# One transformer layer on one core: scatters of routed rows issued earlier, and the first residual sum moved from VectorE to TensorE and ScalarE

## What is computed

```
att = softmax(einsum(zq, zk) / sqrt(rank));  y = (att @ zv) @ U.T
x   = layernorm(x + y @ Wo.T + bo)
top 2 of softmax(x @ gate_w.T), renormalised -> combine
h   = relu(x @ w1.T + b1);  expert_out = h @ w2.T + b2
out = layernorm(x + sum over experts of expert_out * combine)
```

## Time and profile before

| | |
|---|---|
| median of 3 runs | 1260.19 us (1258.29 to 1507.58) |
| the profiled execution's own time | 1257.38 us |
| its span in the trace | 1255.6 us |
| PE / DVE / ACT / POOL busy | 86% / 78% / 72% / 47% |
| attention part | up to about 906 us, bodies b = 0 to 15 |
| routing tail and table | about 906 to 944 us |
| expert part | 944 to 1212 us |
| final layer norms | 1212 to 1256 us |

### The profile page before, as it was taken

One profiled execution on the slowest core, in us unless ns is written; L12 is line 12 of the kernel. 1 busy time (PEld: TensorE's weight loads), 2 busy tenths in 40 slices (PEclk: granted clock), 3 DMA queues, 4 the chain that ended last, 5 costly groups with the idle time before them and its releaser, 6 DMA issues. The chain is left out here.

```text
span 1255.6 us, 24757 instructions
## 1 busy us (share of the span) xinstructions
PE 1082.8 (86%) x7711; PEld 520.5 (41%) x7711; DVE 975.3 (78%) x2117; ACT 904.2 (72%) x1177; POOL 586.5 (47%) x823
## 2 busy tenths in 40 slices
PE   3578998989889898898988999888728999999977
PEld 2222222222222222222222222222218999999952
DVE  4578888989778797887988879797146888888845
ACT  1157877778677786867878678687618999999927
POOL 1314316255271642626336263323254777777745
PEclk9989999999899998989999899899758999999989
DMA  3733133141331413223142231400012222222246
GB/s 80 235 94 90 49 101 89 54 132 42 95 92 51 126 37 106 73 67 102 43 127 69 71 97 36 122 15 19 14 51 63 69 68 69 69 69 71 66 159 257
DMA packets 105461, 104.88 MB, mean 84 GB/s; under 512 B 21608, under 2 KB 82834, under 8 KB 105376
## 3 DMA queue, kind: packets, MB, share of 16 engines
q1 hardware_dynamic: 94912, 81.88, 22.5%
q0 software_dynamic: 8448, 16.93, 4.2%
q10 hardware_dynamic: 2016, 4.98, 1.1%
HBM read 56.06 MB, written 47.39 MB: 82 GB/s over the span
## 5 line engine op out<-in xcount | busy, mean ns | idle before, releaser
L799 DVE TENSOR_REDUCE row_max<-score_ps 128x2 f32<-128x1024 f32 x512 | 618.0, 1220 | 138.9 <-PE score_ps L571 91.3
L685 ACT ACTIVATE probs<-score_ps 128x1024 f32<-128x1024 f32 x512 | 521.6, 1023 | 157.4 <-PE score_ps L553 132.6
L534 PE MATMUL av_ps<-probs,v_one 128*9 128x512 f32 x2048 | 285.2, 630 | 7.9 <-ACT probs L685 6.5
L571 PE MATMUL score_ps<-k_stack,q_stack 48*128 48x512 bf16 x1024 | 207.5, 402 | 75.2 <-ACT probs L685 57.5
L553 PE MATMUL score_ps<-q_stack,k_stack 51*128 51x512 bf16 x1024 | 205.7, 399 | 22.0 <-DVE row_max L799 15.1
L371 POOL TENSOR_TENSOR max_parts<-neg_max,zeros 32x128 bf16<-32x128 f32 x32 | 14.2, 445 | 386.9 <-ACT neg_max L623 386.9
L1096 ACT ACTIVATE w_cur<-experts 128x1156 f32 x136 | 158.5, 1167 | 37.5 <-PEq L413 17.2
L553 PEld LDWEIGHTS score_ps<-q_stack,k_stack 51*128 51x128 bf16 x1024 | 49.2, 93 | 320.4 <-issue 154.2
L1192 POOL DMA_INDIRECT y_d<-y_out,place x136 | 136.8, 1006 | 44.7 <-issue 44.7
L846 POOL DMA_INDIRECT routed_d<-rows,slot_i x128 | 125.4, 980 | 67.2 <-issue 36.9
L1053 PE MATMUL up_ps<-xt_sb,w_cur 128*128 128x128 f32 x1088 | 146.2, 278 | 0.0
(11 more groups left out here) (187 smaller groups left out, 1153.3 us busy)
## 6 DMA issues: line engine op xcount, KB each, us to landing
k_stack<-k_stack_d SPq DMA_DIRECT2D x128, 96.0 KB, 2.4
q_stack<-q_stack_d SPq DMA_DIRECT2D x128, 96.0 KB, 2.5
x_rows_sb<-routed_d SPq DMA_DIRECT2D x136, 65.0 KB
q_stack_d<-q_parts SPq DMA_DIRECT2D x32, 192.0 KB
k_stack_d<-k_parts SPq DMA_DIRECT2D x30, 192.0 KB
x_in<-L_attn_x SPq DMA_DIRECT2D x16, 256.0 KB, 3.1
q_stack_d<-q_parts SPq DMA_DIRECT2D x32, 128.0 KB
x_res<-L_attn_x SPq DMA_DIRECT2D x16, 256.0 KB, 3.1
```

Source lines behind the costliest of these rows:

```text
L534: last = nc.tensor.matmul(av_ps[32 * g:32 * g + V_COLS, :], v_one[n.parity][:, kb, HG * hg + g, :], probs[:, (2 * j + g // 2) % P_RING, g ...
L571: last = nc.tensor.matmul(max_bank(b, s)[:, a, :], q_stack[n.parity][at, c, g * P:(g + 1) * P], k_stack[n.parity][at, c, :], start=True, s ...
L685: nc.scalar.activation(probs[:, s % P_RING, :, :], exp_bank(b, s)[:, :, :], ACT.Exp).then_inc(S["exp_done"], 1)
L799: nc.vector.tensor_reduce(row_max[:, m // (STEPS // 2), :, m % (STEPS // 2)], max_bank(b, s)[:, :, :], AX.X, ALU.max).then_inc(S["red_done ...
```

## The change

Three edits, all in the attention part.

1. **Residual on PE.** At s = 11 PE waits for `xbo_ready` too, and each of the four output projections is followed by a matmul of the identity with `x_bo` into the same PSUM columns, so that the sum is made in `misc_ps`. A new function `residual` on ACT, at s = 12, copies `misc_ps` (128x512) to `res`. DVE's addition goes; its statistics move from s = 12 to s = 13 and the moments from s = 13 to s = 14.
2. **Scatters 0 and 1** of p2 move ahead of `split_max(b, 1)`.
3. **Scatters 2 to 7** of p2 come directly behind `split_max(b, 1)`, ahead of the layer norm's small operations and of `split_q` and `split_k` (where there is a current batch; in the last two bodies they stay at the end).

The diff:

```diff
--- before.py
+++ after.py
@@ -464,8 +464,10 @@
                             if s == 11 and prev:
                                 pe.wait_ge(S["ynt_sb"], p1.count(1, 1))
                                 emptied(s)
+                                pe.wait_ge(S["xbo_ready"], p1.count(1, 1))
                                 for t in range(QT):
-                                    last = nc.tensor.matmul(misc_ps[:, t * P:(t + 1) * P], y_t[:, t * P:(t + 1) * P], wo_t[:, :], start=True, stop=True)
+                                    nc.tensor.matmul(misc_ps[:, t * P:(t + 1) * P], y_t[:, t * P:(t + 1) * P], wo_t[:, :], start=True, stop=False)
+                                    last = nc.tensor.matmul(misc_ps[:, t * P:(t + 1) * P], ident[:, :], x_bo[:, t, :], start=False, stop=True)
                                 last.then_inc(S["wo_done"], 1)
                             if s == 17 and cur:
                                 emptied(s)
@@ -610,8 +612,14 @@
                             wait(act, S["yt_done"], n.count(HG, hg - 1))
                             nc.scalar.activation(y_sb[hg % 2][:, :], av_ps[:, :], ACT.Copy).then_inc(S["y_ready"], 1)
 
+                        def residual(n):
+                            act.wait_ge(S["wo_done"], n.count(1, 1))
+                            wait(act, S["x1_ready"], n.count(QT, 0))
+                            nc.scalar.activation(res[:, :, :].rearrange("p t d -> p (t d)"), misc_ps[:, :], ACT.Copy).then_inc(S["res_ready"], 1)
+
                         def scale_out(n, t):
                             if t == 0:
+                                act.wait_ge(S["res_ready"], n.count(1, 1))
                                 act.wait_ge(S["shift_ready"], n.count(1, 1))
                                 wait(act, scattered[n.parity], n.count_parity(8 * 16, 0))
                             nc.scalar.activation(rows[n.parity][:, 0, t, 0:D], res[:, t, :], ACT.Identity, bias=shift[:, t:t + 1],
@@ -659,6 +667,8 @@
                                 nc.scalar.activation(x1_t[:, :], misc_ps[:, :], ACT.Copy).then_inc(S["x1t_sb"], 1)
                             if s == 10 and cur:
                                 neg(b, 1)
+                            if s == 12 and prev:
+                                residual(p1)
                             if s == 20 and nxt:
                                 act.wait_ge(S["v_done"], n1.count(1, 1))
                                 wait(act, S["av_done"], b.count(STEPS // 2, 0))
@@ -701,11 +711,6 @@
                                                     inv_sum[:, hg, :, :].unsqueeze(3).to_broadcast([P, QT, HG, R]), ALU.mult).then_inc(S["yn_sb"], 1)
 
                         def layernorm(n):
-                            dve.wait_ge(S["wo_done"], n.count(1, 1))
-                            dve.wait_ge(S["xbo_ready"], n.count(1, 1))
-                            wait(dve, S["x1_ready"], n.count(QT, 0))
-                            nc.vector.tensor_tensor(res[:, :, :].rearrange("p t d -> p (t d)"), misc_ps[:, :],
-                                                    x_bo[:, :, :].rearrange("p t d -> p (t d)"), ALU.add).then_inc(S["res_ready"], 1)
                             dve.wait_ge(S["res_ready"], n.count(1, 1))
                             for t in range(QT):
                                 nc.vector.bn_stats(stats[:, t, :], res[:, t, :]).then_inc(S["stats_ready"], 1)
@@ -781,7 +786,7 @@
                                         route(p2, k)
                             if s == 4 and prev:
                                 y_normalise(p1, 3)
-                            if s == 12 and prev:
+                            if s == 13 and prev:
                                 layernorm(p1)
                             if s == 18 and cur:
                                 y_normalise(b, 0)
@@ -789,7 +794,7 @@
                                 y_normalise(b, 1)
                             if s == 30 and cur:
                                 y_normalise(b, 2)
-                            if s == 13 and prev:
+                            if s == 14 and prev:
                                 dve.wait_ge(S["stats_ready"], p1.count(QT, QT))
                             if maximum_at(b, s) is not None:
                                 n, m = Batch(0, maximum_at(b, s) // STEPS), maximum_at(b, s) % STEPS
@@ -853,17 +858,19 @@
                                            base=2 * T * p2.c, channel_multiplier=2).then_inc(S["place_out"], 1)
                         if prev:
                             pool.wait_ge(xres_loaded[p1.parity], p1.count_parity(16, 16))
-                            wait(pool, S["res_ready"], p1.count(1, 0))
+                            wait(pool, S["wo_done"], p1.count(1, 0))
                             nc.gpsimd.tensor_tensor(x_bo[:, :, :], x_res[p1.parity][:, :, :], bo_b[:, :].unsqueeze(1).to_broadcast([P, QT, D]),
                                                     ALU.add).then_inc(S["xbo_ready"], 1)
-                        if cur:
-                            split_max(b, 1)
                         if prev2:
                             pool.wait_ge(S["place_out"], p2.count(1, 1))
                             pool.wait_ge(S["top_step"], p2.count(TOP_STEPS, TOP_STEPS))
                             pool.wait_ge(S["slot_step"], p2.count(SLOT_STEPS, SLOT_STEPS))
                             pool.wait_ge(S["copied"], p2.count(1, 1))
                             scatter(p2, 0, 2)
+                        if cur:
+                            split_max(b, 1)
+                        if prev2 and cur:
+                            scatter(p2, 2, 8)
                         if prev:
                             pool.wait_ge(S["mv_ready"], p1.count(QT, QT))
                             nc.gpsimd.tensor_tensor(var_eps[:, :], mean_var[:, :, 1], eps_t[:, :], ALU.add).then_inc(S["vareps_ready"], 1)
@@ -877,12 +884,10 @@
                         if proj and not is_first(b):
                             split_q(nc.gpsimd, pool, n2)
                             split_k(nc.gpsimd, pool, n2)
-                        if prev2:
-                            scatter(p2, 2, 6)
                         if nxt:
                             split_max(n1, 0)
-                        if prev2:
-                            scatter(p2, 6, 8)
+                        if prev2 and not cur:
+                            scatter(p2, 2, 8)
 
                     schedule(pool, body)
```

## The result

The changed kernel takes 1286.8 us (median of 4 runs, 1282.6 to 1289.2), the kernel before 1261.4; the ratio is 1.021, with a 95% interval of 1.016 to 1.025. The 1261.4 is the median of four runs, one of which took 1507.6 us in a slower state of the chip and counts in no ratio. The forecast was 1286. That the total came out almost exactly is luck: several of its terms were wrong, and their errors cancelled. The profiled execution took 1282.6 us, 25.2 more than the one before.

The account below looks back on a forecast made before the run. The chain through POOL and SP was to bind: 53.0 us plus 1.6 of clock gives 54.6 for bodies 2 to 13, +21; with the other bodies and tail +28.5 on 1257.4, so 1286 us; 8-in-10 range 1261 to 1305.

Parts of the forecast that it names:

- POOL's slip of 3.45 us: POOL's queue behind the six scatters: `var_eps`, `shift`, the q and k parts and the k stores start 3.45 us later.
- The chain from k store to s = 0: From the k stores through SP's queue to the next body's s = 0, which waits for the maxima: 14.93 us.
- The 53.0 us by the chain: Period from s = 0 to s = 0 set by POOL and SP: 49.5 us plus the slip of 3.45.
- PE then sits idle for about 3.3 us at each s = 0: PE waits at s = 0 for the maxima: period 53.0 us less the body's own 49.7.
- PE's own way through the body: The body's own work without the pause: 49.0 us now, about 49.7 with the change, hidden under 53.0.
- I expect the pause at s = 25 to go: Engines' stop near s = 25, about 2.2 us, blamed on scatters running beside k stores; moved scatters would end it.
- rival B: Every s = 0 wait ends in the long clock fall, 3.2 us: 1305 us, chance 0.14; a pause moving with six scatters, nearly the same.
- Its sign for the clock: If PE's rows at s = 0 to 4 stay at 0.39 us, the clock term goes and 1270 us results.
- The clock, 1.6 us a body at s = 0: PE falls to half clock behind its wait at s = 0, lengthening the chain by 1.6 us, bounds 0 and 3.2.
- The sum: Against 1257.4 us: bodies 2 to 13 +21, body 1 +3.5, 14 and 15 +1 each, tail +2; +28.5, 1286 us.
- Residual on PE, +1.1 us, hidden: Four more 128x128 fp32 matmuls at s = 11 add 1.1 us on PE, hidden under the 53.0 us period.
- Rival C: Pause goes and the chain does not bind, so the period is 49.7 us: 1223 us, chance 0.06.

Follow-up runs that it names:

- spread orders: Two kernels: the kernel before with its eight scatters in four pairs, none ahead of the q and k splits, some carried into the next body; 1229.4 and 1230.0 us.
- order 1: Kernel before, scatters in pairs: at s = 8, behind the k split, behind the second split of maxima, behind the next body's bias sum; 1229.4 us, ratio 0.972.
- spread order 2: Kernel before, scatters in pairs: at s = 8, behind the second split of maxima, two pairs carried into the next body; 1230.0 us, ratio 0.975.

## Why the prediction came out, step by step

**POOL's slip of 3.45 us: right.** It measured 3.7; the k stores start 26.25 us behind `y_t` in place of 22.55. The chain from k store to s = 0, 14.93 us by body 1, is 14.0 in body 6 of after (431.65 to 445.66). The 53.0 us by the chain are met in number by bodies 5 and 7 to 9 (53.1 to 53.2). The spread orders confirm the mechanism more strongly than the changed kernel does (the half clock behind the waits is in these costs): a slip of 1.95 us costs 2.3 us a body, one of 2.9 us 3.7, one of 3.7 us (the changed kernel against order 1, which has no stop) 3.2.

**"PE then sits idle for about 3.3 us at each s = 0": wrong.** Instead of twelve waits of 2 to 4 us there are two, of 0.55 and 0.75. PE's own way through the body was taken as 49.7 us, since the stop was to go. It did not go, and with it PE arrives at s = 0 when the maxima do: in body 6 SP's last of six transfers leaves by 444.33 and PE starts at 445.66. In the changed kernel the chain and the stop are two limits of the same size; which of them sets a given body stays open.

**"I expect the pause at s = 25 to go": the failed step.** It left s = 25 but went along with the scatters, from 2.2 us to 3.2 on DVE, and body 14 gained one. The evidence was misread: body 14 of before, with four scatters and no stop, was taken to say that stores must be beside them, while six in a row stop DVE in body 14 too, for 2.84 us. Four are near the border: 0.16 us in body 14, at most 1.24 in spread order 2, 1.9 to 2.4 in before. Why these differ is open. The prediction named this case in rival B's last sentence and under "wrong", but gave it no term. Its sign for the clock went wrong with it: with PE's rows at s = 0 to 4 at 0.39 us, 1270 was to be the result, and it is 1286.8.

**The clock, 1.6 us a body at s = 0: wrong place in this kernel.** Windows of after (stretch, length, PE, PEld, DVE, ACT, POOL busy, granted clock, DMA share, GB/s), in body 10 and in body 14:

```profile
631.00:645.00 14.00, 11.64 (x64) 3.84 (x64) 8.50 (x13) 9.68 (x14) 11.26 (x12) 0.76 0.26 69
645.00:659.00 14.00, 13.13 (x98) 3.97 (x97) 12.33 (x18) 11.02 (x15) 3.06 (x6) 1.00 0.40 113
...
850.00:862.00 12.00, 10.60 (x54) 3.01 (x54) 6.99 (x8) 8.00 (x12) 0.20 (x1) 0.57 0.00 1
```

The lower level (matmuls of 0.61 us for 0.39) follows the stop, not s = 0. The bodies with the most of it take 54.6 to 54.7 us and the others of bodies 2 to 13 52.2 to 53.6; the mean is 53.85, not 54.6. The mechanism itself exists where the chain does bind: in the changed kernel without scatters each of the twelve waits at s = 0 is followed by half clock, and the bodies fall into two kinds, of 51.1 to 52.2 and of 54.3 to 54.8 us. So the clock term failed with the wait that it hung on.

**The sum.** Bodies 2 to 13 brought +12.0 where +21 stood, body 1 +2.3 for +3.5, bodies 14 and 15 +10.6 for +2, start and tail +0.2 for +2: 25.1 for 28.5. The 9 us too many in the twelve bodies and the 8.6 too few in the two last ones cancel. For body 14 the step that failed is again the stop: 2.84 us of it on DVE and 3.80 on PE, and a stretch at a granted clock of 0.57 behind it.

**Residual on PE, +1.1 us, hidden: about right in size, hidden for another reason.** Eight matmuls end 2.05 us behind the first one's start, where four took 1.16, 0.9 us more, and DVE waits 1.3 us for PE at s = 12 in each body. The larger price is the moment later at which POOL may go on, 1.95 us. It shows only where there is no stop: 33.6 us in spread order 1. In the order of before it is 0: there the waits for the maxima, 19.8 us in bodies 2 to 13, come in place of the longer part of PE's stop and of the clock behind it.

**Rival C** (faster if the stop goes and the chain does not bind, 1223 us) is not what the change does, but close to what another order reaches: 1229 and 1230 us, with the stop gone and the q split where it was.

## What to carry to other kernels

Break up indirect DMAs on POOL's queue: in this kernel one or two, then other work of POOL, cost no stop, and six or eight back to back the longest; and keep them from standing ahead of work that another queue's chain is waiting for. Before moving work "into idle time", price what it does to the other engines, not only to its own. When two limits are about equally long, undoing either shows nothing; the residual looked free, and spreading the scatters looked useless beside it, until one of the two was taken away. And a forecast that hits the total has to be compared term by term.

## What the runs showed of the hardware

- A run of indirect DMAs on POOL's queue makes PE, ACT and DVE stand still with inputs made. DVE stood for 0.2 to 2.4 us at four, 2.4 to 3.9 at six and 3.2 to 6.8 at eight; with pairs no such stop is left. Four plain transfers of the same rows from the same queue, done in 2.2 us, do not stop them, and four scatters of 8-byte rows do as much as those of 520. By what means a run of scatters stops the other engines no run here shows.
- An indirect scatter of 128 rows holds POOL for 0.98 us on average, at 8 bytes a row as at 520, a plain transfer of the same rows for 0.55.
- A wait of 1.75 to 2.8 us for a DMA was followed by half clock on PE in all twelve bodies of the changed kernel without scatters; a stop of 2.97 us in body 2 of before was not the earlier trace rows.
- Leaving out 112 of the 128 scatters, all of which run beside other work, shortened the kernel by 55 us.
